# Centring on GpSimd by one two-input subtraction for two groups, and one multiplication for each group, in a 30-step feed-forward loop

## The reference

```python
def step(h, _):
    h = h + 0.01 * jnp.tanh(h)
    h = h * jax.nn.sigmoid(h)
    h = _layernorm(h, ln_w, ln_b)
    h = jnp.einsum('bsc,dc->bsd', h, W) + b
    return (h, None)
x, _ = jax.lax.scan(step, x, None, length=N_ITERS)   # N_ITERS = 30
...
x = x + _L0_gnn_ref(_layernorm(x, axis=-1), adj, L0_gnn_W, L0_gnn_b)
x = x + _L0_ffn_ref(_layernorm(x, axis=-1), L0_ffn_weight, L0_ffn_bias)
x = x + _L1_gnn_ref(...)
x = x + _L1_ffn_ref(_layernorm(x, axis=-1), L1_ffn_ln_w, L1_ffn_ln_b, L1_ffn_W, L1_ffn_b)
```

## Time and profile before

| what | value |
|---|---|
| median of 3 runs | 1288.19 us (1287.89 to 1288.37) |
| profiled execution | 1290.16 us, its span 1288.3 us |
| TensorE busy | 1250.8 us, 97% of the span, 9315 instructions |
| VectorE busy | 1156.3 us, 90%, 3029 instructions |
| ScalarE busy | 960.1 us, 75%, 1170 instructions |
| GpSimd busy | 991.9 us, 77%, 1867 instructions |
| mean granted TensorE clock | 0.994 of full speed |

### The profile page before, as it was taken

How to read it: one execution, slowest core, us unless ns; L and a number is a source line. 1 busy time by engine, 2 the same in 40 slices (tenths; PEclk the granted TensorE clock), 3 DMA queues, 4 the chain that set the end, 5 groups by cost and what they waited for, 6 DMA issues and landing times.

```text
span 1288.3 us, 30559 instructions
## 1 busy us (share of the span) xinstructions
PE 1250.8 (97%) x9315; PEld 1111.1 (86%) x9315; DVE 1156.3 (90%) x3029; ACT 960.1 (75%) x1170; POOL 991.9 (77%) x1867
## 2 busy tenths in 40 slices
PE   8899999999999999789999999999999999999998
PEld 7677777777777777589999999999999999999998
DVE  7888888888888877889999999999999999999996
ACT  2455555555555555789999999999999999999994
POOL 3455555554555554699999999999999999999997
PEclk9999999999999999889999999999999999999999
DMA  6111111111111000000000000000000000000004
GB/s 192 42 42 44 52 52 53 45 41 41 41 41 41 0 1 1 1 2 1 0 0 0 0 0 0 0 0 0 0 0 0 0 0 0 0 0 0 0 0 131
DMA packets 29811, 27.75 MB, mean 22 GB/s; under 512 B 3285, under 2 KB 21464, under 8 KB 29656
## 3 DMA queue, kind: packets, MB, share of 16 engines
q1 hardware_dynamic: 29784, 27.41, 6.6%
HBM read 23.21 MB, written 4.19 MB: 21 GB/s over the span
## 4 chain that ended last, share of the span: by engine, by line
PE 39%; DVE 5%; issue 5%; POOL 4%; ACT 2%; DVEq 0%; POOLq 0%; ACTq 0%
PE psum L890 24%; PE psum L942 13%; POOL h_ring L528 3%; PE psum L906 3%; ACT t_ring L1010 2%; DVE f_stat L1309 2%; POOL h_ring L525 1%; DVE u_ring L1326 1%; DVE f_share L1363 1%; DVE psum L1368 1%; DVE psum L1379 0%; DVE psum L1382 0%; DVE f_rs L1397 0%; DVEq L1307 0%; DVEq L1320 0%
## 5 line engine op out<-in xcount | busy, mean ns | idle before, releaser
L528 POOL TENSOR_SCALAR h_ring<-g_ring,f_less,f_rs 128x128 f32<-128x128 f32 x960 | 428.1, 457 | 0.0
L1309 DVE BATCH_NORM_STATS2 f_stat<-g_ring 128x6 f32<-128x256 f32 x960 | 393.6, 424 | 2.4 <-ACT g_ring L1000 2.4
L942 PE MATMUL psum<-ident,h_ring 128*128 128x128 f32 (+1 forms) x1920 | 339.6, 279 | 9.6 <-POOL h_ring L528 9.4
L525 POOL TENSOR_TENSOR h_ring<-g_ring,f_rs 128x256 f32<-128x256 f32 x480 | 296.1, 617 | 17.5 <-DVE f_rs L1397 15.4
L1326 DVE SCALAR_TENSOR_TENSOR u_ring<-t_ring,psum 128x1024 f32<-128x1024 f32 x232 | 282.9, 1219 | 28.2 <-ACT t_ring L1010 27.0
L890 PE MATMUL psum<-w_t,y_all 128*128 128x128 f32 x1920 | 293.7, 276 | 0.0
L890 PE MATMUL psum<-w1c_t,y_all 128*128 128x128 f32 x1920 | 293.7, 276 | 0.0
L942 PEld LDWEIGHTS psum<-ident,h_ring 128*128 128x128 f32 (+1 forms) x1920 | 254.2, 167 | 43.4 <-POOL h_ring L528 17.0
L1010 ACT ACTIVATE t_ring<-psum 128x1024 f32<-128x1024 f32 x232 | 237.7, 1025 | 43.1 <-PE psum L890 42.8
L1014 ACT ACTIVATE y_all<-psum 128x1024 f32<-128x1024 f32 x240 | 244.0, 1017 | 15.9 <-PE psum L942 15.9
L890 PEld LDWEIGHTS psum<-w1c_t,y_all 128*128 128x128 f32 x1920 | 253.9, 193 | 0.0
(11 more groups left out here) (201 smaller groups left out, 2189.8 us busy)
## 6 DMA issues: line engine op xcount, KB each, us to landing
work<-in_adj_dram SPq DMA_DIRECT2D x16, 1024.0 KB, 5.5
x_tok<-in_x_dram SPq DMA_DIRECT2D x16, 256.0 KB, 5.6
out_dram<-y_all SPq DMA_DIRECT2D x7, 512.0 KB, 3.2
work<-in_L_gnn_conv_w_dram SPq DMA_DIRECT2D x1, 1088.0 KB
out_dram<-y_all SPq DMA_DIRECT2D x2, 256.0 KB, 3.6
work<-in_L_gnn_w_ih_dram SPq DMA_DIRECT2D x1, 384.0 KB
work<-in_L_gnn_w_hh_dram SPq DMA_DIRECT2D x1, 192.0 KB
work<-in_L_gnn_W_dram SPq DMA_DIRECT2D x1, 64.0 KB, 5.1
```

The costliest lines, as they stand in the source:

```text
L525: pool.tensor_tensor(tiles(h_ring[j % 4])[:, first:first + PLAIN, :], tiles(g_ring[j])[:, first:first + PLAIN, :], spread(f_rs[:, both(j), ...
L528: ins = pool.tensor_scalar(tiles(h_ring[j % 4])[:, t, :], tiles(g_ring[j])[:, t, :], f_less[:, j, t:t + 1], f_rs[:, both(j), at + t:at + t ...
L942: m = pe.transpose(g_ps[j % 2][0:rows, t // NT, P * (t % NT):P * (t % NT) + P], tiles(h_ring[j % 4])[:, t, 0:rows], ident[:])
L1309: ins = dve.bn_stats(f_stat[:, j, 0, 2 * q:2 * q + 2, :].rearrange("p t w -> p (t w)"), two)
```

## The change

`less_mean`, f_less and the tensor-scalars are gone, and with them PLAIN. In each group one half is centred as a whole (`centred(j)`: half j % 2) and the other not at all. `centre` subtracts the means from the centred halves of both groups of a pair, in place in g_ring, by one two-input instruction over 2 x 512 columns; the buffers of a pair now lie side by side (g_pair), so that the two halves, the first quarter and the last of the pair's 2048 columns, are one access pattern. `scale` multiplies the 1024 columns of a group by f_rs in one two-input instruction and raises f_norm once. In a GpSimd slot `scale` now comes ahead of `centre`, where `less_mean` came ahead of `scale`.

```diff
-            def less_mean(j, s):
+            def centre(j, s):
                 pool.wait_ge(f_bn, s + 2)
-                settle(pool, s_passed_pool)
-                pool.tensor_scalar(f_less[:, j:j + 2, :], f_stat[:, j:j + 2, 0, :, 1], -1.0, 1.0,
-                                   ALU.mult, ALU.mult).then_inc(f_mean, 1)
+                two = g_pair[j // 2][:].rearrange("p g n -> p (g n)").rearrange("p (q n) -> p q n", n=N)[:, 0:4:3, :] \
+                    .rearrange("p g (t c) -> p g t c", c=C)
+                means = f_stat[:].rearrange("p g o t w -> p (g o t) w")[:, :, 1].rearrange("p (q t) -> p q t", t=NT)[:, 4 * j:4 * j + 6:5, :] \
+                    .rearrange("p g (t o) -> p g t o", o=1).broadcast_to([P, 2, NT, C])
+                pool.tensor_tensor(two, two, means, ALU.subtract).then_inc(f_mean, 1)
...
                 wait(pool, f_turn, s - 3)
-                for h in (j % 2, 1 - j % 2):
-                    first = NT * h
-                    at = GT * (j % 2)
-                    pool.tensor_tensor(tiles(h_ring[j % 4])[:, first:first + PLAIN, :], tiles(g_ring[j])[:, first:first + PLAIN, :],
-                                       spread(f_rs[:, both(j), at + first:at + first + PLAIN], PLAIN, C), ALU.mult)
-                    for t in range(first + PLAIN, first + NT):
-                        ins = pool.tensor_scalar(tiles(h_ring[j % 4])[:, t, :], tiles(g_ring[j])[:, t, :],
-                                                 f_less[:, j, t:t + 1], f_rs[:, both(j), at + t:at + t + 1], ALU.add, ALU.mult)
-                    ins.then_inc(f_norm, 1)
+                at = GT * (j % 2)
+                pool.tensor_tensor(tiles(h_ring[j % 4]), tiles(g_ring[j]),
+                                   spread(f_rs[:, both(j), at:at + GT], GT, C), ALU.mult).then_inc(f_norm, 1)
...
             def slot(it, k):
-                older = earlier(it, k, LAG_M)
-                if older is not None and k % 2 == 0:
-                    less_mean(*older[1:])
                 before = earlier(it, k, LAG_P)
                 if before is not None:
                     scale(*before)
+                newer = earlier(it, k, LAG_M)
+                if newer is not None and k % 2 == 0:
+                    centre(*newer[1:])
...
-                    pe.wait_ge(f_norm, 2 * s + 1)
+                    pe.wait_ge(f_norm, s + 1)
                 for n in range(GT):
                     if before is not None:
                         if n == NT:
-                            pe.wait_ge(f_norm, 2 * s + 2)
-                            wait(pe, f_state, s)
-                        t = (n + NT * (j % 2)) % GT
-                        rows = P if t % NT < PLAIN else P - 1
+                            if ends(i, 0) and j == 0:
+                                pe.wait_ge(s_x_nmp_lo, B)
+                            else:
+                                pe.wait_ge(f_state, s)
+                        t = (n + NT * centred(j)) % GT
+                        rows = P - 1 if n < NT else P
```

More of the change, by code:

```diff
@@ L56 @@
 EARLY = 7
-PLAIN = 2
 SEED_SLOPE = -0.5
@@ L113, in build @@
         f_rs = sb("f_rs", [P, 2, PAIR])
-        f_less = sb("f_less", [P, GROUPS, GT])
         f_share = sb("f_share", [P, PAIR])
@@ L197, in build @@
         u_ring = [sb(f"u_ring{r}", [P, GN])[:] for r in range(2)]
-        g_ring = [sb(f"g_ring{r}", [P, GN])[:] for r in range(4)]
+        g_pair = [sb(f"g_pair{r}", [P, 2, GN]) for r in range(2)]
         h_ring = [sb(f"h_ring{r}", [P, GN])[:] for r in range(4)]
-        g_ring += [sb(f"g_ring{r}", [P, GN])[:] for r in range(4, GROUPS)]
+        g_pair += [sb(f"g_pair{r}", [P, 2, GN]) for r in range(2, GROUPS // 2)]
+        g_ring = [g_pair[j // 2][:, j % 2, :] for j in range(GROUPS)]
         psum = ctx.enter_context(nc.psum_tensor("psum", [P, 8, N], F32))
@@ L403, in both, with centred @@
             return j // 2 % 2
+        def centred(j):
+            return j % 2
         def pairs(i, j):
@@ L582, in step @@
                     power(3)
-                    less_mean(2, 2)
+                    centre(2, 2)
                 if l1:
@@ L595, in step @@
                     power(0)
-                    less_mean(0, 0)
+                    centre(0, 0)
                     scale(0, 0, 0)
@@ L890, in product_group @@
                         m = pe.matmul(y_ps[k % 2][:, h, C * t:C * t + C], y_all[:, GT * k + NT * h + t, :],
-                                      w1_t[:] if t < PLAIN else w1c_t[:], start=False, stop=True, skip_group_check=True)
+                                      w1c_t[:] if h == centred(k) else w1_t[:], start=(h == centred(k) and t == 0), stop=True, skip_group_check=True)
                     if h == 0 and ends(it, ITERS) and k == GROUPS - 1:
@@ L903, in bias_free, with bias @@
                     pe.wait_ge(f_u, it * GROUPS + k)
[L905 to L908, removed]
+            def bias(k, part):
+                pe.matmul(y_ps[k % 2][:, 1 - centred(k), 2 * C * part:2 * C * part + 2 * C], ones_bf[:],
+                          bias1[:, 0:2, :].rearrange("p t c -> p (t c)"),
+                          start=(part == 0), stop=False, skip_group_check=True)
             def ones_row(b):
-                for t in range(0, NT, NT - PLAIN):
-                    pe.matmul(bank[b][:, C * t:C * t + C * (NT - PLAIN)], ones_bf[:],
-                              bias1[:, PLAIN:NT, :].rearrange("p t c -> p (t c)"), start=(t == 0), stop=True,
+                for t in range(0, NT, 2):
+                    pe.matmul(bank[b][:, C * t:C * t + 2 * C], ones_bf[:],
+                              bias1[:, 2:4, :].rearrange("p t c -> p (t c)"), start=(t == 0), stop=True,
                               skip_group_check=True)
@@ L926, in slot @@
                         ones_row(CONV)
-                        pe.wait_ge(s_x_nmp_lo, B)
-                        ones_row(CHAN)
                     elif ends(i, 0) and j == 1:
@@ L946, in slot @@
                             bias_free(it, k)
-                        bias(k, n // NT)
+                        bias((k + 1) % GROUPS, n // NT)
                 if before is not None:
@@ L1162, in _ @@
             link(dve.memset(bias1[:], 0.0))
-            dve.memset(bias1[0:1, PLAIN:NT, :], 1.0)
+            dve.memset(bias1[0:1, 2:4, :], 1.0)
             dve.memset(b1_cols, 0.0)
@@ L1248, in split_bias @@
                 link(dve.tensor_copy(part_bf[:, 2, :], part_f[:, 2, :]))
-                for t in range(PLAIN):
+                for t in range(2):
                     for r in range(3):
@@ L1395, in root_link @@
                     dve.wait_ge(f_link, done)
-                    dve.wait_ge(f_norm, 2 * s - 4)
+                    dve.wait_ge(f_norm, s - 2)
                     dve.scalar_tensor_tensor(out=f_rs[:, both(j), :], in0=f_share[:], scalar=LESS[2],
```

## The result

The changed kernel takes **1267.09 us** (median, 1266.1 to 1268.01) beside 1288.04 (1287.67 to 1288.37) for the kernel before on the same chip: a ratio of 0.9837, with an interval of 0.982 to 0.9854. It is faster, as forecast, and lies in the range; it is 12 us slower than the 1255 that the likeliest case gave. The profiled execution took 1266.86, its span is 1265.1 where it was 1288.3.

A forecast was written before the change was run, and what follows sets the result against it. GpSimd's throughput and the delay from f_rs to a group's last tile were taken to bound the loop; 28 x (24.44 - 23.25) = 33.3 us off 1290.16 leaves 1256.9, scaled to the median 1255; range 1249 to 1297.

The forecast's parts named there:

- likeliest case: Whole kernel: an iteration falls from 24.44 to 23.25 us over 28 full iterations, giving 1255 us; chance 0.68.
- The bound: Feed-forward loop: TensorE waits 1.32 us an iteration, for second halves of groups, by GpSimd's throughput and the delay from f_rs.
- step called doubtful: GpSimd's 1024-column operations: access, not length, decides the price, so each takes 1.87 us.
- turning point: GpSimd: up to 1.93 us for one operation (5.78 / 3), its exact price costs nothing.
- Rival A: GpSimd: length counts, so both new operations cost the 512-column rows' price, 27.9 us an iteration, 1386 us; chance 0.19.
- Rival B: GpSimd: only centre is dear, working in place on two separated halves; a pair takes 6.04, about 1290 us; chance 0.09.
- A pair on GpSimd: Two scales and one centre take 3 x 1.855 = 5.57 us instead of 5.96, 22.3 an iteration.
- The thin slack: TensorE's wait for a whole group: ready at 7.35 us, wanted at 7.57, slack 0.22; 0.13 an iteration allowed with the branch.
- The sum: Loop: GpSimd 22.3, TensorE 23.12, VectorE just under; 23.25 an iteration, saving 33.3 us over 28 iterations.
- the hand-over: Before the loop: ones and 0.2 of f_less go, a centre of 1.87 comes twice: 0 to +3 us.
- Rival C: GpSimd is freed without gain: TensorE's stall moves to f_rs, the next late thing; about 1287 us; chance 0.04.
- Waits for f_rs once in each pair: Expected sign in GpSimd's profile after, with its busy share falling from 98% to about 96% of a shorter iteration.

The follow-up runs named there:

- centre aside: Changed kernel with VectorE's loop begun one slot later, and centre in the loop writing to an unread buffer, so scale doesn't wait for it: 1257.21 us, single timing.
- jump moved by one slot: Changed kernel with VectorE's loop begun one slot later, so its branch stands behind a slot that has just issued f_rs: 1260.8 us, ratio 0.9789 to the kernel before.

## Why the prediction was right, and where it was off

- **The bound.** Right. TensorE waited for GpSimd's second halves; with one operation for a group its quiet slots stay at 2.89, so that the other order of tiles and weights costs nothing, and no stall is left ahead of the second four transposes. How much of the 0.88 is GpSimd's pace and how much the shorter delay to a group's second half, no run separates.
- **The price.** The step called doubtful held: 1.90 and 1.91 us, where 1.87 was taken and 1.93 was the turning point. Rival A (1386) needed 2.34; the run with a moving second input, where two operations of a pair's three cost that, takes 1365.81. Rival B falls with centre's 1.91; writing in place costs nothing that can be seen. The Trainium skill's rule (GPSIMD Engine Reference, section 3.1), by whose half 1024 columns were estimated at 2.25, comes near the moving input (2.368) and not the one that stands still (1.898). By the rival's own sum, 2.25 makes 1355 to 1360, not the 1363 given there.
- **A pair on GpSimd.** Mis-sized: 5.57 was said, 5.79 measured. 0.06 are the prices. 0.16 to 0.21 are idle time that the prediction put at nothing: centre was said to stand "in what is idle time there", but it fills the queue until f_rs comes, and scale starts 0.235 after that at the earliest. The second of its two waits costs 0.16 an iteration (centre aside).
- **The thin slack.** This is the step that failed: "the 0.13 pays for the thin slack and the loop's branch". The slack of 0.22 adds the 3.05 from product to u of one slot (901.33 to 904.38) and the 2.03 from u to f_rs of another (923.06 to 925.09). The other is the slot with the jump, and there u comes 3.25 after its product (919.81 to 923.06), which leaves a slack of 0.02. After the change it comes 3.41 after: 3.41 + 2.03 + 0.39 + 1.90 = 7.73 is later than the 7.57 at which TensorE wants the group, and TensorE loses 0.20 by the jump (jump moved by one slot). The 7.57 is a little late too, since the tiles of h are loaded as weights ahead of their transposes (the waits are PEld's): without the jump the group is ready 7.5 after its product, and the slot still takes 3.00.
- **The sum.** 0.32 of the 0.44 lie in the slot of the late pair, 0.11 in the one four slots later. 0.20 go with the jump, 0.16 with the second wait, and 0.08 are left. The runs agree: without the jump 23.36, without centre 23.40, without jump and wait 23.20. In the last of these VectorE is busy all the time, so that its own work, put at 23.04, is more likely 23.2 and what is left. 23.56 in place of 23.25 makes 28 x 0.31 = 8.7 of the 12 us, and the hand-over, put at 0 to +3 and left out of the sum, 1.4 with the first and the last iteration. The other 2 are no work: the profiled execution of before lay 2.0 above its median (1290.16 to 1288.19), which the forecast scaled down, and that of after (1266.86) lies at its median.
- **Rival C** had the mechanism of what was left: f_rs is the next late thing. It had the size wrong, taking all of the gain where a quarter went. "Waits for f_rs once in each pair" came nearer than the list of waits shows: it names f_rs once in each iteration, but f_rs decides when scale starts in three pairs of four.

## What to carry to other kernels

When the engine that holds the others gets faster and several are above 95% busy, don't add up busy time only: work out the delay from each producer to its consumer for the worst slot, the one with a loop's jump in it, and compare it with the slack. Take each term of that delay from that slot, and not from a neighbour. A releaser in a profile is what ended last; whether it decided is seen from the distance to the start, which stays the same behind the one that does. And a wait takes time on its queue even when what it waits for is there, so what comes last shouldn't have a second wait behind it (the two waits of scale in the other order were not run). A cost that was worth nothing before a change (here the place of a jump, 0.9991 before and 6 us after) is to be tried again behind it.

## What the runs showed of the hardware

- A two-input operation of GpSimd costs 1.66 ns a column where the second input stands still for 128 columns, and 2.12 where it moves by one column at each element, at the same 1024 columns.
- GpSimd starts an instruction 0.160 us after the end of VectorE's f_rs where that is all it waits for, and 0.235 after it where a second wait stands behind, for a semaphore that is already up. After its own last instruction, where it waits for that one's semaphore, it starts at 0.16 at the least; without a wait the next one starts some 0.04 before the end that the trace gives.
- VectorE's jump back over one or two iterations of its loop takes its sequencer 0.3 us from the branch to the next record, over four iterations 2.8. The engine stands still for it (0.2 and 2.7 us) where nothing is queued, and not at all where the jump was moved by one slot.
